# Two-layer graph network: an order of work changed on four engines, and VectorE in place of POOL for the rounding rest of the row tiles

## The chip, the cores and the metric

One NeuronCore of a Trainium2 chip runs the whole program. The metric is the device time of one execution in microseconds (us). Engines are named as in the profile: PE (TensorE; PEld is its weight load), DVE (VectorE), ACT (ScalarE), POOL (GpSimd), SP (the queue that issues the DMAs).

## The reference

```python
edge_index = jnp.stack([src, dst])                     # 80000 edges, 2500 nodes, D = 1024, f32
h = jnp.maximum(_layernorm(x, axis=-1), 0.0)
x = x + _L0_gnn_ref(h, L0_gnn_W, edge_weight, src, dst)
h = jnp.maximum(_layernorm(x, axis=-1), 0.0)
x = x + _L1_gnn_ref(h, edge_index, L1_gnn_W, L1_gnn_b)

# layer 0: support = h @ W; out = segment_sum(support[src] * edge_w[:, None], dst)
# layer 1: edges plus one self loop for each node; h' = h @ W.T + b;
#          deg = number of edges by row; norm = deg^-0.5[row] * deg^-0.5[col];
#          out = segment_sum(norm[:, None] * h'[col], row)
```

`dst` is sorted; `src` is random.

## The kernel before, in words

Both layers are done as dense f16 products, with every operand split into a rounded half and the rest ("first" and "second" part), so that three products give nearly f32. The 2500 rows are 20 row tiles (t = 0 to 19) of 128.

**Layer 0, first half: "supports" and "quads".** For each row tile, PE computes `support(t, k0, k1)`: 8 blocks k of 6 matmuls 128x512 (L1688). Between blocks 1 and 2 it turns the next row tile (`transpose_rows(t + 1)`, L1671, 16 transposes), which needs the rounded half of it (ACT, `rows_normal`, L1470) and the rest, h minus its rounded half (`h_left`, L737, on POOL, counted by `h_ready`). From t = STEP0 = 4 on a tile also carries a quad w = t - 4: sums of one-hot products (L1700) that turn the edge list into dense blocks of the weighted adjacency and of the edge counts. A quad has 8 one-hot steps (w = 0), 4 (w = 1, 2), 3 (w = 3 to 8) or 2 (from w = 9). For a step, POOL fills `fbuf` (L769, L771; `fields_of`), DVE compares and multiplies it into `slots` (L1055 to L1061; `hots_of(w, i0, i1)`, two buffers), and PE multiplies. At a quad's end ACT copies the sums out (L1418 to L1420), DVE makes the second part (L1124 to L1128, `early_second_part`) and SP parks the result in DRAM. In these tiles DVE also does `sup_left` (L962, the support's rest), `split_left` (L1136, the rest of W1 at 2^n scale, t = 4 to 11), `moments` and `scale_shift` of later row groups (L873 to L887), and the table of what edges each later window holds: `own_select` (t = 7, 8 and 10 to 15), `select_windows` (t = SELECT_AT = 9) and `later_windows` (t = TABLE_AT = 16), each of them a chain of small instructions at a tile's end. PE's part of the table is `tables(t)`, after block 5. W1's scale needs its largest absolute row sum: ACT sums (`weight_sums(1, k)`, L1497), DVE reduces (L1032), PE turns it (`spread_max(2, ...)`, L1631), DVE reduces again (L1232), PE spreads it (`to_all(3, ...)`, L1636), DVE makes the power of two.

**Layer 0, second half.** For each target tile, 120 matmuls of adjacency by support (L1801) in 8 groups, the next tile's quads between them.

**Layer 1.** SP loads x1, layer 0's output, in groups of 4 row tiles (`load_x1`, L597) and the edge counts, turned on the way (`load_first_parts`, L587, first parts in `area`; `load_second_parts`, L592, in `etab` and `slots`). ACT makes relu of the norm (L1609), ACT or DVE the rounded half, DVE the rest (`split`, L1302, `h2_ready`). PE: `sums_of_first` for column chunk c = 0 (320 matmuls, L1888), then `products(0)` (L1948), then `sums` and `products` for c = 1 to 4. DVE's `sums2_left` (L1345) makes the sums' second part, on which `products` waits; `norms` (L1363, L1365) is 40 multiply-adds into `s_acc`, one for each of 20 first and 20 second parts of the counts, on which PE waits (`acc_ready`) after the first output tile.

Every engine's program is written out by hand, in order, with semaphores; nothing is reordered.

Of the kernel before, what the change touches and what calls it, by code (L numbers as in the profile page):

```python
# [6 lines left out]
def gnn_two_layers(nc, x, src, dst, edge_weight, w0, w1, b1, out):  # L7
# [5 lines left out]
    P = 128  # L13
# [56 lines left out]
    with ctx:  # L70
# [394 lines left out]
        def _(sp):  # L465
# [62 lines left out]
            for w in range(PQ):  # L528
# [12 lines left out]
                if w + STEP0 == TABLE_AT + 1:  # L541
                    sp.wait_ge(own_ready, len(OWN_AT))
                    sp.wait_ge(table_ready, 2)
                    fetch_parked(0)
# [78 lines left out]
            load_first_parts(0, 0)  # L623
            for s in range(2):
                sp.wait_ge(x1_out[s], 16 * last)
            for k in range(4):
                sp.wait_ge(sup_free, k + 1)
                load_x1(k)
                load_first_parts(0, k + 1)
                if k == 0:  # L630
# [7 lines left out]
            store_x1(last, 1, LAST)  # L638
            sp.wait_ge(x1_out[1], 16 * (T // 2))
# [53 lines left out]
        def _(pool):  # L693
# [120 lines left out]
            for t in range(STEP0, T):  # L814
                if t + 2 < T:
                    h_left(t + 2)
# [40 lines left out]
        def _(dve):  # L857
# [135 lines left out]
            sup_left(1)  # L993

# [3 lines left out]
            def passes(a, b, count, cum, spare, start=None):  # L998
# [7 lines left out]
                if start is not None:  # L1006
                    chain(nc.vector.tensor_scalar(cum, cum, start, None, ALU.add))
                for v0, v1, per, n0 in ((a, min(b, VB), QPT, a // QPT), (max(a, VB), b, 4, QB)):
# [12 lines left out]
            passes(0, VA, n_row[:, 0:VA], wcum[:, 0:VA], wtmp0)  # L1021
# [7 lines left out]
            moments(3)  # L1029
            scale_shift(3)  # L1030
            dve.wait_ge(w1_summed, KD)
            nc.vector.tensor_reduce(top[:, 3:4], w_sums[:, 1, :], AX.X, ALU.max).then_inc(top_ready, 1)  # L1032
            regs = [dve.alloc_register(f"dve_window{i}") for i in range(2)]
# [105 lines left out]

            def support_share(w):  # L1140
                if w in MOMENTS_AT:
                    moments(MOMENTS_AT[w])
# [83 lines left out]
            def later_windows():  # L1226
                chain(nc.vector.tensor_copy(wcum[:, 0:NA], tab[:, 1, VA:NW]))
                passes(VA, NW, wcum[:, 0:NA], wcum[:, 0:NA], wtmp, top[0:1, 10:11])

            hots_of(0)  # L1230
            dve.wait_ge(top_tp, 3)
            nc.vector.tensor_reduce(top[0:1, 5:6], bank[0][0:1, 0:P], AX.X, ALU.max).then_inc(top_row, 1)  # L1232
            dve.wait_ge(top_all, 3)
            powers(bank[1][:, 0:1], 0, 1)
            nc.vector.tensor_scalar(scale_of[:, 0:1], sc[:, 8:9], 2.0 ** 13, None, ALU.mult).then_inc(w_pow, 1)
            for w in range(PQ):
                hots_of(w, 1, 2) if w > 0 else None
                sup_left(w + STEP0 - 1)
                hots_of(w, 2, 8)
                for g in W1_AT.get(w + STEP0, ()):  # L1240
                    split_left(g)
                if w + STEP0 == HOTS_AT:
                    chunk_one_hots()
                further(w, 2)
# [4 lines left out]
                if w + STEP0 in OWN_AT:  # L1249
                    own_select(w + STEP0)  # L1250
                if w + STEP0 == SELECT_AT:
                    select_windows()
                if w + STEP0 == TABLE_AT:
                    later_windows()
# [95 lines left out]
            def norms(c, k0, k1):  # L1350

                for k in range(k0, k1):
                    if k % HK == 0:
                        dve.wait_ge(cthi_in[k // HK], 16 * (c + 1))
                    if k % LK == 0:
                        dve.wait_ge(ctlo_in[k // LK], 16 * (c + 1))
                    for part_of in (ct_hi_of, ct_lo_of):
# [10 lines left out]
                if k1 == T:  # L1368
# [24 lines left out]
            dve.wait_ge(b_in, 16)  # L1393
            for c in range(NCK):
                step = T // KD + 1
                if c == 0:
                    norms(c, 0, T - 6)
                for f in range(KD):
                    sums2_left(c, f)
                    if c > 0:  # L1400
                        norms(c, min(T, step * f), min(T, step * (f + 1))) if step * f < T else None
                if c == 0:
                    norms(c, T - 6, T)
# [4 lines left out]
        def _(act):  # L1408
# [130 lines left out]
            for t in range(T):  # L1539
# [14 lines left out]
                if t in (2, 3):  # L1554
                    act.wait_ge(w1nat_in, 16)
                    for k in range((t - 2) * KD // 2, (t - 1) * KD // 2):
# [68 lines left out]
        def _(pe):  # L1625
# [205 lines left out]
            for t in range(T):  # L1831
                w = t - STEP0
                quad = 0 <= w < PQ
                support(t, 0, 2)
                if t + 1 < T:
                    transpose_rows(t + 1)
                if w == 0:
                    pe.wait_ge(ranges_ready, 2)
# [150 lines left out]
```

## Time and profile before

| | |
|---|---|
| median of 3 runs | 1492.66 us (1488.78 to 1494.58) |
| the profiled execution | 1490.92 us, of which 1489.1 us is the span from its first to its last instruction |
| mean granted TensorE clock | 0.989 of full speed |
| busy share of the span | PE 96%, PEld 57%, DVE 60%, ACT 34%, POOL 30% |
| first row tile to the last quad | 31 to 327 us of the span |
| layer 0's second half | 327 to 917 us |
| layer 1 | 926 us to the end |

[...] A PE line with an idle time in brackets says how long PE stood before it and who released it. Matmul durations in a merged row are those of the group, modelled ends included.

### The profile page before, as it was taken

To read this page: it belongs to the slowest core of one execution; us is meant where nothing else is said; L and a number is where in the kernel's file an instruction comes from. 1 tells how busy PE (TensorE), PEld (TensorE's weight loads), DVE (VectorE), ACT (ScalarE), POOL (GpSimd) and SP (SyncE) were. 2 spreads that over 40 slices of the span, in tenths; PEclk is the share of its full clock that TensorE was granted. 3 is DMA by queue.
4 is the path that set the end of the run, shared out by engine and by line. 5 is a ranking of instruction groups with operands and counts; after the bars stand their busy time and mean duration, and the time that the engine had idled before them with its cause. 6 is when DMAs were issued, how large, how long until landed. Compare 5 with 4: busy or idle time off the path is not lost.

```text
span 1489.1 us, 23949 instructions
## 1 busy us (share of the span) xinstructions
PE 1424.4 (96%) x7586; PEld 846.5 (57%) x7587; DVE 899.7 (60%) x1804; ACT 507.8 (34%) x922; POOL 453.1 (30%) x865
## 2 busy tenths in 40 slices
PE   3989999999999999999999997989999999999999
PEld 2445455456666666666676664446446446446455
DVE  7788785653777776677767662873552452542542
ACT  7545555522444445455455541610000000000000
POOL 2247565432555555555555550000000000000000
PEclk9999999999999999999999998999999999999999
DMA  8303443251544535454545558937308008017002
GB/s 308 114 20 60 105 89 36 28 83 49 97 79 71 96 72 104 86 96 80 109 75 92 100 95 139 264 91 155 98 9 217 29 19 206 29 33 193 29 2 83
DMA packets 427818, 139.14 MB, mean 93 GB/s; under 512 B 397705, under 2 KB 409993, under 8 KB 427669
## 3 DMA queue, kind: packets, MB, share of 16 engines
q1 hardware_dynamic: 427669, 137.43, 42.0%
q8 instruction: 60, 0.98, 0.3%
q14 instruction: 89, 0.73, 0.2%
HBM read 53.46 MB, written 53.52 MB: 72 GB/s over the span
## 4 chain that ended last, share of the span: by engine, by line
PE 67%; issue 12%; DVE 6%; SPq 5%; POOL 4%; DMA 2%; POOLq 2%; ACT 1%; ACTq 0%; DVEq 0%
PE pair L1801 24%; PE pair L1888 18%; PE pair L1948 14%; PE pair L1688 6%; PE pair L1700 4%; SPq L587 3%; DVE own_w L1365 1%; POOLq L766 1%; DMA h<-in_L_gnn_W 1%; SPq L592 1%; POOL deg_acc L787 1%; POOL fbuf L769 1%; POOL fbuf L771 1%; DMA x_scratch<-xt 1%; POOL fbuf L780 1%
## 5 line engine op out<-in xcount | busy, mean ns | idle before, releaser
L1801 PE MATMUL pair<-h,area 128*128 128x512 f16 x2400 | 542.7, 379 | 0.0
L1801 PEld LDWEIGHTS pair<-h,area 128*128 128x128 f16 x2400 | 342.9, 147 | 147.3
L1888 PE MATMUL pair<-area,h 128*128 128x500 f16 x1600 | 340.7, 376 | 9.6 <-DVE h L1302 9.4
L1888 PEld LDWEIGHTS pair<-area,h 128*128 128x128 f16 x1600 | 157.0, 98 | 192.5 <-issue 13.6
L787 POOL TENSOR_TENSOR deg_acc<-deg_acc,area 128x320 f32<-128x320 f32 x160 | 139.7, 873 | 276.0 <-DVE area L1124 274.5
L1948 PE MATMUL pair<-wmat,area 128*125 128x512 f16 x960 | 211.5, 382 | 4.5 <-DVE area L1345 4.5
L1418 ACT ACTIVATE area<-pair 128x320 f32<-128x320 f32 x160 | 70.1, 438 | 329.8 <-PE pair L1700 327.6
L1622 ACT ACTIVATE area<-pair,sc 128x500 f16<-128x500 f32 x40 | 27.1, 677 | 450.0 <-PE pair L1888 450.0
L1948 PEld LDWEIGHTS pair<-wmat,area 128*125 128x125 f16 x960 | 131.7, 138 | 81.7 <-issue 7.3
L792 POOL TENSOR_TENSOR aux<-area,aux 128x320 f16<-128x320 f32 x144 | 147.6, 1025 | 0.0
L1700 PE MATMUL pair<-slots 128*128 128x120 f16 (+1 forms) x1152 | 112.5, 235 | 20.4 <-DVE slots L1061 18.0
L1055 DVE TENSOR_TENSOR slots<-iota_r,fbuf 128x320 f16<-128x320 f16 (+1 forms) x145 | 60.6, 418 | 116.2 <-POOL fbuf L781 47.5
L1425 ACT ACTIVATE aux<-area 128x320 f16<-128x320 f32 x144 | 126.4, 878 | 0.1
L1700 PEld LDWEIGHTS pair<-slots 128*128 128x128 f16 x1152 | 84.7, 99 | 67.5 <-DVE slots L1061 34.7
L1688 PE MATMUL pair<-wmat,aux 128*128 128x512 f16 x480 | 116.0, 391 | 3.1 <-DVE wmat L949 3.1
L1688 PE MATMUL pair<-wmat,xt 128*128 128x512 f16 x480 | 113.1, 386 | 0.3 <-DVE h L962 0.3
L1128 DVE TENSOR_TENSOR area<-area 128x320 f16<-128x320 f16 x160 | 109.6, 685 | 5.5
L1124 DVE TENSOR_TENSOR area<-area 128x16 f16 (+1 forms) x160 | 32.8, 205 | 115.6 <-ACT area L1420 114.6
L1345 DVE SCALAR_TENSOR_TENSOR area<-pair,sc,area 128x500 f16<-128x500 f32 x40 | 28.9, 737 | 120.2 <-ACT area L1622 120.2
L1057 DVE TENSOR_TENSOR slots<-iota_r,fbuf 128x1024 f16<-128x1024 f16 x145 | 99.7, 688 | 0.0
L1688 PEld LDWEIGHTS pair<-wmat,aux 128*128 128x128 f16 x480 | 46.4, 100 | 54.3 <-issue 8.5
L1125 DVE SCALAR_TENSOR_TENSOR area<-pair,area 128x320 f16<-128x320 f32 x160 | 76.8, 480 | 0.0
(208 smaller groups left out, 1263.4 us busy)
## 6 DMA issues: line engine op xcount, KB each, us to landing
c_scratch<-aux SPq DMA_DIRECT2D x72, 320.0 KB, 4.5
xt<-in_x SPq DMA_DIRECT2D x19, 512.0 KB, 3.6
x_scratch<-xt SPq DMA_DIRECT2D x19, 512.0 KB, 4.7
xt<-x_scratch SPq DMA_DIRECT2D x20, 448.0 KB
out_x<-xt SPq DMA_DIRECT2D x19, 448.0 KB
h<-x_scratch SPq DMA_DIRECT2D x4, 2048.0 KB, 10.3
h<-in_x SPq DMA_DIRECT2D x5, 1024.0 KB, 6.2
h<-in_L_gnn_W SPq DMA_DIRECT2D x4, 1024.0 KB, 11.4
```

The costliest lines, as they stand in the source:

```text
L787: pool.tensor_tensor(deg_acc[:], deg_acc[:], c_stage(s), ALU.add).then_inc(win_sum, 1)
L792: pool.tensor_tensor(second_parts, by_source(c_stage(s)), first_parts, ALU.subtract).then_inc(c_lo, 1)
L1057: nc.vector.tensor_tensor(part(to, 0, P), columns(8, P), by_touch(s, 1, 8, P), ALU.is_equal)
L1125: nc.vector.scalar_tensor_tensor(by_window(parts[:, 1], r), sums_in(pair, r, 1), A_DOWN, by_window(parts[:, 0], r), ALU.mult, ALU.subtract ...
L1128: nc.vector.tensor_tensor(parts[:, 1], parts[:, 1], seconds, ALU.add).then_inc(win_lo, 1)
L1418: act.activation(by_window(c_stage(s), r), sums_in(pair, r, 0), ACT.Copy, scale=C_DOWN)
L1425: act.activation(to, by_source(c_stage(s)), ACT.Copy).then_inc(c_hi, 1)
L1688: last = pe.matmul(dest[:, half * H:(half + 1) * H], h_t(t)[:, q, k, :], wmat[:, r, k, half * H:(half + 1) * H], start=k == q == r == 0, s ...
L1700: return pe.matmul(dest, touches[:, t, 0:P], touches[:, t, P:], start=first, stop=last, skip_group_check=True)
L1801: last = pe.matmul(sum_pair(e)[:, half * H:(half + 1) * H], wts(e)[:, q, :, k], hpart(k, r)[:, half * H:(half + 1) * H], start=k == q == r ...
L1888: ins = pe.matmul(sums_of(c, f), hpart(k, q)[:, f * P:(f + 1) * P], counts, start=first and q == 0, stop=last and q == 1, skip_group_check ...
L1948: last = pe.matmul(out_pair(m)[0:RW, half * H:(half + 1) * H], agg_of(k, q)[:, b * RW:(b + 1) * RW], wmat[:, r, k, half * H:(half + 1) * H ...
```

## The change

It reorders work on SP, DVE, ACT and PE and moves one operation from POOL to DVE. The diff is cut: of `passes`, only how it is divided is shown.

```diff
@@ SP, quads
-                if w + STEP0 == TABLE_AT + 1:
+                if w + STEP0 == TABLE_AT + 2:
                     sp.wait_ge(own_ready, len(OWN_AT))
                     sp.wait_ge(table_ready, 2)
                     fetch_parked(0)
@@ SP, end of layer 0
             sp.wait_ge(c_out[1], 32 * (T - PRE))
-            load_first_parts(0, 0)
             for s in range(2):
                 sp.wait_ge(x1_out[s], 16 * last)
             for k in range(4):
                 sp.wait_ge(sup_free, k + 1)
                 load_x1(k)
-                load_first_parts(0, k + 1)
-                if k == 0:
+                load_first_parts(0, k)
+                if k == 1:
                     sp.wait_ge(deg_out, 16)
...
             load_x1(4)
             store_x1(last, 1, LAST)
+            load_first_parts(0, HJ - 1)
@@ POOL, quads
             for t in range(STEP0, T):
-                if t + 2 < T:
-                    h_left(t + 2)
@@ DVE, before the quads
             sup_left(1)
+            moments(3)
...
-            def passes(a, b, count, cum, spare, start=None):
+            def steps_each(a, b, count, cum, spare, start=None):
...
+            def steps_by_quad(a, b, cum, spare):
...
             for t in range(2, STEP0 - 1):
                 sup_left(t)
-            moments(3)
-            scale_shift(3)
             dve.wait_ge(w1_summed, KD)
             nc.vector.tensor_reduce(top[:, 3:4], w_sums[:, 1, :], AX.X, ALU.max).then_inc(top_ready, 1)
+            scale_shift(3)
...
+            def h_left(t):
+
+                dve.wait_ge(relu_ready, 2 * t + 2)
+                dve.wait_ge(ht_tp, 2 * (t - 1))
+                dve.wait_ge(h_ready, t)
+                nc.vector.tensor_tensor(hs(t)[:, 1, :], h[:, t, :], hs(t)[:, 0, :], ALU.subtract).then_inc(h_ready, 1)
...
+            def table_share(t):
+
+                if t in OWN_AT:
+                    own_select(t)
+                if t == SELECT_AT:
+                    select_windows()
+                if t == TABLE_AT:
+                    chain(nc.vector.tensor_copy(wcum[:, 0:NA], tab[:, 1, VA:NW]))
+                    steps_each(VA, NW, wcum[:, 0:NA], wcum[:, 0:NA], wtmp, top[0:1, 10:11])
+                if t == TABLE_AT + 1:
+                    steps_by_quad(VA, NW, wcum[:, 0:NA], wtmp)
@@ DVE, quads
-            hots_of(0)
             dve.wait_ge(top_tp, 3)
             nc.vector.tensor_reduce(top[0:1, 5:6], bank[0][0:1, 0:P], AX.X, ALU.max).then_inc(top_row, 1)
+            hots_of(0, 0, 1)
             dve.wait_ge(top_all, 3)
...
+            hots_of(0, 1, 2)
             for w in range(PQ):
                 hots_of(w, 1, 2) if w > 0 else None
                 sup_left(w + STEP0 - 1)
                 hots_of(w, 2, 8)
+                table_share(w + STEP0 - 1)
                 for g in W1_AT.get(w + STEP0, ()):
                     split_left(g)
                 if w + STEP0 == HOTS_AT:
                     chunk_one_hots()
+                if w + STEP0 + 2 < T:
+                    h_left(w + STEP0 + 2)
                 further(w, 2)
                 if w + 1 < PQ:
                     hots_of(w + 1, 0, 1)
                 early_second_part(w)
                 support_share(w)
-                if w + STEP0 in OWN_AT:
-                    own_select(w + STEP0)
-                if w + STEP0 == SELECT_AT:
-                    select_windows()
-                if w + STEP0 == TABLE_AT:
-                    later_windows()
@@ DVE, layer 1 (norms takes parts: first, second or both)
-            dve.wait_ge(b_in, 16)
+            norms(0, 0, T, (ct_hi_of,))
             for c in range(NCK):
                 step = T // KD + 1
-                if c == 0:
-                    norms(c, 0, T - 6)
                 for f in range(KD):
                     sums2_left(c, f)
-                    if c > 0:
-                        norms(c, min(T, step * f), min(T, step * (f + 1))) if step * f < T else None
+                    if c == 0:
+                        norms(c, f, f + 1, (ct_lo_of,))
+                    elif step * f < T:
+                        norms(c, min(T, step * f), min(T, step * (f + 1)))
                 if c == 0:
-                    norms(c, T - 6, T)
+                    norms(c, KD, T, (ct_lo_of,))
+                    dve.wait_ge(b_in, 16)
@@ ACT
-                if t in (2, 3):
+                if t == 2:
                     act.wait_ge(w1nat_in, 16)
-                    for k in range((t - 2) * KD // 2, (t - 1) * KD // 2):
+                    for k in range(KD):
                         weight_sums(1, k)
@@ PE
                 support(t, 0, 2)
+                if w == 0:
+                    to_all(3, bank[1][:, 0:1], 5, 6)
                 if t + 1 < T:
                     transpose_rows(t + 1)
-                if w == 0:
-                    pe.wait_ge(ranges_ready, 2)
-                    spread_max(2, P, 3)
                 for k in range(2, KD):
                     support(t, k, k + 1)
...
+                    if w == -1 and k == 5:
+                        pe.wait_ge(ranges_ready, 2)
+                        spread_max(2, P, 3)
                     if w == 0 and k == 2:
-                        to_all(3, bank[1][:, 0:1], 5, 6)
                         pe.wait_ge(table_ready, 1)
```

## Rows read from the trace of the kernel before

**Rows 1.** Busy time by stretch: PE, PEld, DVE, ACT, POOL, granted clock, DMA share, GB/s
```profile
84.00:124.00 40.00, 33.86 (x234) 18.68 (x233) 32.28 (x82) 16.98 (x28) 20.82 (x57) 0.91 0.10 32
124.00:168.00 44.00, 44.00 (x309) 23.81 (x308) 36.24 (x72) 25.05 (x38) 30.11 (x73) 1.00 0.50 108
...
285.00:305.00 20.00, 15.12 (x87) 7.32 (x86) 19.50 (x35) 7.91 (x13) 11.89 (x29) 0.91 0.44 84
```

**Rows 2.** Who PE waited for, 84 to 330 us: total us, times, longest
```profile
PE pair L1700 <- DVE slots L1061: 13.3, 5, 4.9
```

**Rows 3.** PE in order of time, quads: start, us, line, operands, count, idle before
```profile
90.15 0.38 PE L1636 MATMUL pair<-top,ones 1*128 1x1 f32 x2 [1.23 <-DVE top L1232]
...
91.90 2.77 PE L1688 MATMUL pair<-wmat,aux 128*128 128x512 f16 x6
...
105.64 0.98 PE L1700 MATMUL pair<-slots 128*128 128x120 f16 x8 [2.98 <-DVE slots L1061]
106.71 3.74 PE L1688 MATMUL pair<-wmat,xt 128*128 128x512 f16 x12
...
194.85 0.98 PE L1700 MATMUL pair<-slots 128*128 128x120 f16 x8 [3.14 <-DVE slots L1061]
...
299.39 0.59 PE L1700 MATMUL pair<-slots 128*128 128x120 f16 x8 [4.88 <-DVE slots L1061]
```

**Rows 4.** DVE in order of time, before and in the quads
```profile
75.98 0.24 DVE L1020 CAST area<-area 1x128 int32<-1x128 f32 x1 [4.65 <-DMA area<-wsmall]
...
80.80 4.82 DVE L873 BATCH_NORM_STATS2 stats<-h 128x6 f32<-128x512 f32 x8
...
102.32 2.17 DVE L1055 TENSOR_TENSOR slots<-iota_r,fbuf 128x320 f16<-128x320 f16 x1 [0.32 <-POOL fbuf L771]
...
186.04 0.35 DVE L1219 TENSOR_SCALAR area<-area 128x768 f16<-128x768 f16 x1
...
191.65 2.25 DVE L1060 TENSOR_TENSOR slots<-slots,fbuf 128x320 f16<-128x320 f16 x1
...
287.79 0.66 DVE L1227 CAST area<-area 1x768 f32<-1x768 int32 x1
...
296.90 1.17 DVE L1017 TENSOR_TENSOR area<-area 1x768 int32<-1x768 f32 x1
```

**Rows 5.** POOL in order of time: the first of 14 subtractions from t = 6 on
```profile
102.20 2.12 POOL L737 TENSOR_TENSOR aux<-h,aux 128x1024 f16<-128x1024 f32 x1
```

**Rows 6.** DVE's groups by line and shape, 915 to 1000 us: busy us, mean ns
```profile
L1302 DVE TENSOR_TENSOR h<-aux,h 128x1024 f16<-128x1024 f32 x10 | 12.2, 1224 | 0.2
...
L1365 DVE SCALAR_TENSOR_TENSOR own_w<-area,dinv,own_w 128x500 f32<-128x500 f16 x13 | 9.6, 739 | 0.7
```

**Rows 7.** PE in order of time, layer 1: column chunks 0 and 1
```profile
926.52 70.32 PE L1888 MATMUL pair<-area,h 128*128 128x500 f16 x320 [9.44 <-DVE h L1302]
1001.37 13.05 PE L1948 MATMUL pair<-wmat,area 128*125 128x512 f16 x48 [4.52 <-DVE area L1345]
...
1046.45 67.63 PE L1888 MATMUL pair<-area,h 128*128 128x500 f16 x320
1113.92 10.52 PE L1948 MATMUL pair<-wmat,area 128*125 128x512 f16 x48
```

**Rows 8.** SP's queue in order of time, end of layer 0: start, us of issue
```profile
895.17 0.43 SPq L619 DMA_DIRECT2D deg_scratch<-deg  x1
896.08 9.19 SPq L587 DMA_TRANSPOSE area<-c_scratch  x1
905.39 0.70 SPq L597 DMA_DIRECT2D h<-x_scratch  x1
```

**Rows 9.** DMA issues, 894 to 934 us: count, size, us from issue to landing
```profile
deg_scratch<-deg SPq DMA_DIRECT2D x1, 10.0 KB, 20.1
```

**Rows 10.** ACT in order of time, layer 1's first instruction
```profile
922.72 1.24 ACT L1609 ACTIVATE area<-h,shift,scale 128x1024 f32<-128x1024 f32 x1 [25.93 <-DMA h<-x_scratch]
```

**Rows 11.** DVE in order of time, the first of the 40 sums for `s_acc`
```profile
978.25 0.48 DVE L1363 TENSOR_SCALAR own_w<-area,dinv 128x500 f32<-128x500 f16 x1 [9.41 <-DMA area<-in_L_gnn_b]
```

More of the change, by code:

```diff
@@ L1007, in passes @@
                     chain(nc.vector.tensor_scalar(cum, cum, start, None, ALU.add))
+            def steps_by_quad(a, b, cum, spare):
+                n = b - a
                 for v0, v1, per, n0 in ((a, min(b, VB), QPT, a // QPT), (max(a, VB), b, 4, QB)):
@@ L1020, in _ @@
             chain(nc.vector.tensor_copy(tab[:, 0, 0:VA], lo_row[:, 0:VA]))
-            passes(0, VA, n_row[:, 0:VA], wcum[:, 0:VA], wtmp0)
+            steps_each(0, VA, n_row[:, 0:VA], wcum[:, 0:VA], wtmp0)
+            steps_by_quad(0, VA, wcum[:, 0:VA], wtmp0)
             chain(nc.vector.tensor_copy(top[0:1, 10:11], wcum[:, VA - 1:VA]))
@@ L1224, in select_windows @@
                 dve.sem_inc(left_ready, 1)
-            def later_windows():
-                chain(nc.vector.tensor_copy(wcum[:, 0:NA], tab[:, 1, VA:NW]))
-                passes(VA, NW, wcum[:, 0:NA], wcum[:, 0:NA], wtmp, top[0:1, 10:11])
-            hots_of(0)
+            def table_share(t):
[8 more added lines that the diff above has]
+                    steps_by_quad(VA, NW, wcum[:, 0:NA], wtmp)
             dve.wait_ge(top_tp, 3)
             nc.vector.tensor_reduce(top[0:1, 5:6], bank[0][0:1, 0:P], AX.X, ALU.max).then_inc(top_row, 1)
+            hots_of(0, 0, 1)
             dve.wait_ge(top_all, 3)
@@ L1348, in _, with norms @@
             accs = [0]
-            def norms(c, k0, k1):
+            def norms(c, k0, k1, parts=(ct_hi_of, ct_lo_of)):
                 for k in range(k0, k1):
-                    if k % HK == 0:
+                    if k % HK == 0 and ct_hi_of in parts:
                         dve.wait_ge(cthi_in[k // HK], 16 * (c + 1))
-                    if k % LK == 0:
+                    if k % LK == 0 and ct_lo_of in parts:
                         dve.wait_ge(ctlo_in[k // LK], 16 * (c + 1))
-                    for part_of in (ct_hi_of, ct_lo_of):
+                    for part_of in parts:
                         counts = part_of(k)
@@ L1367, in norms @@
                         ins.then_inc(acc_step, 1)
-                if k1 == T:
+                if k1 == T and ct_lo_of in parts:
                     dve.wait_ge(acc_step, accs[0])
```

## Prediction

> **What bounds the kernel now.** I read the page first: PE is busy nearly all the time, so the time is PE's matmuls plus the places where PE stands. A change of order can only pay at those places. So the second view is busy time by stretch, to find them [rows 1]: from 124 to 168 us PE works all 44.00 us at full clock (1.00), from 84 to 124 it works 33.86 of 40.00 (6.1 idle), from 285 to 305 it works 15.12 of 20.00 (4.9 idle), and both carry a mean granted clock of 0.91, that is, a part of the stretch at 1.2 instead of 2.4 GHz. The third view, who PE waited for [rows 2], puts 13.3 us of the quads on DVE's one-hots. The fourth, PE in order of time [rows 3], gives the single places: 1.23 us for W1's scale, 2.98 at 105.64, 3.14 at 194.85, 4.88 at 299.39. Before and after each, matmuls are slow: 6 products take 2.77 us, 12 take 3.74, where chunk 1 does 48 in 10.52 [rows 7], so 1.3 and 2.6 are their length. So a stall costs itself and 1.0 to 1.5 us at the lower clock. The listed four make 12.2 us, the waits of [rows 2] and the scale's 14.5; with three small ones of 1 us or less the idle time is 16.6, and with the slow stretches (four of 1.0 to 1.5) about 22 us.
>
> Layer 1's beginning has two more places [rows 7]: PE stands 9.44 us before the first sums and 4.52 before the first products; the 320 sums take 70.32 instead of chunk 1's 67.63, the 48 products 13.05 instead of 10.52. That is 12.1 + 7.0 = 19.2 us. The ceiling of the whole change is thus 22 + 19 = 41 us.
>
> **Quads: what holds DVE.** A one-hot instruction of 128x320 took 2.17 us at 102.32 and 2.25 at 191.65 [rows 4]; its like in the same group take 0.3. POOL's subtraction stood beside the first of them, 102.20 to 104.3 [rows 5]. So DVE's instructions with both operands in SBUF wait until POOL's is over. There are 14 of these (t = 6 to 19), each able to cost DVE up to 1.9 us. The change takes them away and gives DVE 14 subtractions of its own; the same shape, f32 and f16 in, f16 out, takes 1.224 us on DVE [rows 6], 17 us in all, against up to 27 saved. DVE is busy 36.2 of 44 us in [rows 1], so it has no large reserve: what counts is where the 1.2 us lie.
>
> The Trainium skill (SBUF — State Buffer, section on the two separate sides) says that DVE and GpSimd share one port pair, held exclusively for a whole instruction, also by a DVE instruction with two SBUF inputs; the trace agrees in DVE's 2.17 us. By that rule the moved subtraction in its turn blocks POOL 1.2 us.
>
> **The tiles one by one**, walked with PE's tile as fixed work (8 blocks of 1.3 us, transposes 0.9, 0.42 a one-hot step, 1.6 to 4.3 the table) and DVE's list in its new order:
>
> *t = 3.* DVE's 4.65 us before 75.98, a wait for a DMA, are filled by the 4.82 us of `moments(3)` [rows 4]; the chain behind comes 0.8 us later, and W1's maximum is ready at about 82 instead of 87.2. `spread_max` now stands after block 5, which PE reaches at 80.2: a new wait of 1.8 us. ACT does 4 more weight sums (1.04 each) in t = 2, so its rows of t = 5 come 2 us later, at 81; PE needs them at 87.7. Covered.
>
> *t = 4.* The scale's wait of 1.23 and its neighbours (1.0 and 0.9) go: `to_all` comes 5 us after its operand. Eight steps end the tile; the last three stand at block 7 and each must wait for its one-hots (1.55 us for four instructions, two buffers), so of the 2.98 us about 1.2 stay. From 82.73 to 106.71 the tile took 24.0; now 18.9 with the wait of t = 3 in it: 5 us, and 1.0 more because the 12 products at 106.71 run at full clock.
>
> *t = 5 to 8.* No wait before, none now: DVE's subtraction for t + 2 is done 0.6 to 2 us before PE's transposes, closest in t = 5.
>
> *t = 9 to 12.* The select chain, from 186.04 to nearly 191 us [rows 4], stood ahead of a one-hot that PE waited 3.14 us for. It now lies in tile 10 behind all of that tile's one-hots. But `own_select(8)` is now inside tile 9, and PE's `tables(9)` waits for it: about 1.3 us. In tile 11, DVE is late from `moments(5)`, another 1.3. The old waits there (1.6 and 3.14, with the slow products behind) made tiles 9 and 10 6.6 us longer than their work; 2.6 are lost again: 4.0.
>
> *t = 13 to 19.* The table of later windows, from 287.79 to 298 [rows 4], stood before the one-hot of the 4.88 us wait. Its first half (about 5 us) goes to tile 17, its second (4, of which POOL's lock is 1.8) to tile 18, both behind the one-hots, where DVE idled for about 6 us a tile. The 4.88 us and about 1.8 of slow products go: 6.7, and 1.2 in tile 13. SP's `fetch_parked(0)` now waits in t = 18 until about 9 us into it; the fetch lands 5 us later, with 9 us left before PE uses it. SP's queue holds `park_counts(13)` back behind it; ACT waits for that, not PE.
>
> Sum: 6.0 + 4.0 + 7.9 = 17.9. I take 15.5, since the two or three new waits of over 1 us may also bring slow products (1 each). Bounds: 9 (the new waits twice as long and slow ones at each) and 20.
>
> **End of layer 0.** SP spends 9.19 us issuing the first transpose of counts before the first load of x1, 896.08 to 905.39 [rows 8]; ACT starts on it at 922.72 after 25.93 us of waiting [rows 10], and PE 3.8 us later. PE's last matmul of layer 0 ends at 917.1. Now the load goes out at about 896.4, when PE has freed the first four blocks. What is unknown is how fast it is: the write of the counts' sums (`deg_scratch`, 10 KB in 4-byte pieces) stands before it in the queue and takes 20.1 us to land, until 915.3 [rows 9]; in that time the transpose trickled too. Lower bound: the load is finished by 905 and PE starts at 917.3, all 12.1 us come back. Upper: nothing moves before 915 and 2 MB at 5 us more land at 920, PE starts at about 924, 2.7 come back. I take 914 for the landing: PE starts at 917.7, waits about 1.5 us more in pieces for the first splits (DVE 1.9 us each), 9.5 to 10 come back. The later loads: SP now waits for the write's landing before x1's third group, at 915; that group lands by 921 and PE wants it at about 945. The stall goes, and DVE's splits are next: 33 us of work in PE's 67. Covered.
>
> Here the skill speaks against it: DMA: Bandwidth & Descriptors, section Specifications, has pieces under 512 B done as read-modify-write; by that rule the write stays slow and in front of the load. That is the second rival below.
>
> **First products.** DVE waited 9.41 us for the bias [rows 11], which it doesn't need for the sums. 28 of the 40 then run at 0.775 us (0.739 and the step, [rows 6]) ahead of `sums2_left(0, 0)`. Now 20 (15.5 us) follow the last split. That ends at about 957 to 960, so they end by 975, and PE gives the first finished sum at about 975. No wait is left: 7.0 us come back. Then 20 second parts, 8 between the `sums2_left` and 12 behind (9.3 us), end at about 996.5; PE reaches that wait at 996. So 0.5 is given back: 6.5.
>
> Sum here 9.5 + 6.5 = 16, from 9 to 19.
>
> POOL's `fields_of`, now no longer queued behind a wait for ACT's rows, the bias wait and `scale_shift(3)` behind the maximum are costed at nothing: POOL's fields wait for DVE's one-hots anyway, the bias lands 17 us before `finish(0)`, and t = 8's rows are needed 30 us later. Without that cover `scale_shift(3)` would cost its 0.5.
>
> **Total.** 15.5 + 16 = 31.5 off the profiled 1490.9 gives 1459.4; the runs' median lies 1.7 above the profiled one, so 1461.
>
> **The rivals.**
> 1. *DVE is too full* (chance 0.17). For: 36.2 of 44 us busy [rows 1], and now 1.2 us more a tile in a row with the chains ahead of it, so that PE's transposes wait in t = 6 to 12. Against: the 2 us waits for POOL go. 1 us in each of 7 tiles: 1468.
> 2. *The first load stays behind the small write* (0.20): landing at 920. 6.5 us of the 9.5 are lost: 1467 to 1468.
> 3. *Both orders find other covers, nothing moves* (0.05): the one-hots' two buffers already set the quads and the loads the rest. Against it stand the 9.44 us. 1490.
> 4. *Slower* (0.03): the subtraction on DVE stands behind a one-hot that waits for PE, which waits for the transposes. It closes a loop that lasts the tile. It decides once each of 14 tiles grows by over 2.25 us (31.5 / 14), DVE's lateness in t = 5 being 2.9 us from where I put it; at 3 us a tile it is 1461 + 42 = 1503.
> 5. The forecast (0.55): 1461, own range 1453 to 1467.
>
> Faster by over 0.5% (7.5 us, about what a measurement of this kernel tells from no change): 0.92; within: 0.05; slower: 0.03. The range is 1452 to 1474: the low end is the ceiling, 41 us off the median of the runs, and the high end takes in rivals 1 and 2 together (1461 + 7 + 6.5).
>
> **What would show it.** No DVE one-hot of over 1.5 us between 100 and 300; the last quad's product at about 310 instead of 327; PE's waits for one-hots under 5 us instead of 13.3; a new PE wait of 1 to 2 us for the maximum near 80 and one in tile 9. The first sums within 3 us of layer 0's end, 67 to 69 us long, the products right behind. It would be wrong if PE's transposes (L1671) wait for DVE, if the load lands after 918, or if the granted clock stays at 0.91 though the waits are gone.

## The result, and the profile after

| | before | after |
|---|---|---|
| median (lowest to highest), 4 runs each | 1493.04 us (1488.78 to 1494.58) | 1466.67 us (1462.03 to 1469.22) |
| the profiled execution and its span | 1490.92, 1489.1 us | 1462.03, 1460.2 us |
| mean granted TensorE clock | 0.989 | 0.998 |

The ratio is 0.9826, with a 95% interval of 0.9801 to 0.9851: faster by 1.7%, or 26.4 us between the medians. The profiled execution after is the fastest of its four, so the spans differ by a little more, 28.9 us, and the account below is of the spans.

Busy time by stretch, after (columns as in [rows 1]):
```profile
84.00:124.00 40.00, 38.37 (x301) 22.12 (x300) 34.35 (x87) 21.81 (x31) 22.38 (x62) 1.00 0.16 37
...
285.00:305.00 20.00, 20.00 (x130) 10.48 (x129) 9.93 (x25) 5.98 (x11) 6.56 (x20) 1.00 0.64 102
```
The two stretches in which PE idled 6.1 and 4.9 us have 1.6 and 0 idle, and the granted clock is 1.00 in both, where it was 0.91.

Who waited for whom, after, 84 to 300 us (total us, times, longest), the answer to [rows 2]:
```profile
POOL fbuf L769 <- DVE slots L1064: 41.3, 22, 5.7
...
PE pair L1717 <- DVE slots L1064: 1.1, 1, 1.1
...
DVE slots L1058 <- POOL fbuf L771: 0.6, 2, 0.3
```
PE's wait for one-hots fell from 13.3 to 1.1 us. The third row has this one for its like in the kernel before, same view and stretch:
```profile
DVE slots L1055 <- POOL fbuf L771: 26.3, 11, 6.1
```
DVE waited 26.3 us for POOL's fields, now 0.6, and it is POOL that waits for a buffer.

PE in order of time, quads, after (columns as in [rows 3]):
```profile
69.51 2.75 PE L1705 MATMUL pair<-wmat,xt 128*128 128x512 f16 x12 [0.25 <-DVE h L960]
...
79.77 0.27 PE L1648 MATMUL pair<-ident,top 128*1 128x128 f32 x1 [1.44 <-DVE top L1034]
...
98.41 0.59 PE L1717 MATMUL pair<-slots 128*128 128x120 f16 x8 [1.15 <-DVE slots L1064]
...
172.30 0.38 PE L1752 MATMUL pair<-area 128*128 128x512 f16 x1 [1.99 <-DVE area L1222]
...
307.21 26.06 PE L1818 MATMUL pair<-h,area 128*128 128x512 f16 x120
```
Three of the waits forecast are there, near the sizes forecast, and 4.88 and 3.14 are gone. Tile 3 begins at 69.51 where it began at 71.48 before; in the other kernels below it begins between 69.5 and 70.8. From there to the first product of the second half it is 237.7 us, before 255.9 (71.48 to 327.39): 18.2 less.

PE in order of time, layer 1, after, beside [rows 7]:
```profile
903.26 56.25 PE L1906 MATMUL pair<-area,h 128*128 128x500 f16 x256 [6.00 <-DVE h L1318]
...
960.25 13.67 PE L1906 MATMUL pair<-area,h 128*128 128x500 f16 x64 [0.74 <-issue]
973.75 10.52 PE L1966 MATMUL pair<-wmat,area 128*125 128x512 f16 x48
985.52 1.03 PE L1975 MATMUL pair<-ones,own_w 128*125 128x1 f32 x8 [1.25 <-DVEq L1386]
986.42 31.27 PE L1966 MATMUL pair<-wmat,area 128*125 128x512 f16 x144
```
The products follow the sums without a gap, at full clock. The first sums still start 6.00 us after layer 0's last matmul (897.26), and they take 70.7 us from first to last, 70.3 before. From layer 0's end to the products' second part it was 98.2 us (917.1 to 1015.3) and is 89.2 (897.26 to 986.42): 9.1 less.

The account: 2.0 from the earlier start, 18.2 in the quads, 9.1 at layer 1's start make 29.3; 0.4 is lost in layer 0's second half (590.1 us for 589.7). The forecast had 15.5 and 16 for the two terms. Not all of the 29.3 is the change's: the earlier start of tile 3 stands in kernels without the new orders too (69.5 and 69.6 in experiments 3 and 4), and 3.4 of the 9.1 went with a write that landed 3.4 us sooner in this execution, as shown below.

SP's queue, after, the answer to [rows 8]:
```profile
875.24 0.43 SPq L619 DMA_DIRECT2D deg_scratch<-deg  x1
876.27 2.16 SPq L597 DMA_DIRECT2D h<-x_scratch  x1
878.49 20.68 SPq L587 DMA_TRANSPOSE area<-c_scratch  x1
```
ACT in order of time, after, layer 1's first instruction, the answer to [rows 10]:
```profile
899.45 1.24 ACT L1626 ACTIVATE area<-h,shift,scale 128x1024 f32<-128x1024 f32 x1 [22.50 <-DMA h<-x_scratch]
```
DMA, 874 to 914 us, after: what was moved in each of 40 slices of 1 us, and the write's landing, the answer to [rows 9]:
```profile
GB/s 156 178 383 180 15 0 0 45 16 33 20 49 57 16 33 53 66 53 66 176 414 410 399 251 89 227 231 242 389 418 426 406 277 217 191 3 3 31 90 393
...
deg_scratch<-deg SPq DMA_DIRECT2D x1, 10.0 KB, 16.7
```
The load is the second row of SP's queue, issued at 876.3, right behind the write of 10 KB. While the write is under way the engines move at most 66 GB/s from 878 on; it lands at 891.9, in the slice from 894 they move 414, and the 2 MB are there by 899.4. The load was brought forward, and what it had waited for before, it waited for again: ACT starts 7.5 us behind the write's landing here, and started 7.4 behind it before (915.3 to 922.72).

### The profile page after: what moved, and what is told of

Same layout as the page of the kernel before. It is cut to its first block, busy times and chain, and to the rows that moved or that the text cites. A ratio compares the mean times of both kernels' runs of the same rounds, so it can differ in the third digit from the quotient of the medians.

```text
span 1460.2 us, 23951 instructions
## 1 busy us (share of the span) xinstructions
PE 1413.4 (97%) x7586; PEld 842.6 (58%) x7587; DVE 898.2 (62%) x1818; ACT 507.6 (35%) x922; POOL 438.7 (30%) x851
## 4 chain that ended last, share of the span: by engine, by line
PE 81%; issue 8%; DVE 5%; DMA 2%; POOL 2%; ACT 1%; SPq 0%; POOLq 0%; ACTq 0%; DVEq 0%
PE pair L1818 25%; PE pair L1906 23%; PE pair L1966 13%; PE pair L1705 12%; PE pair L1717 4%; DMA h<-x_scratch 2%; PE pair L1765 1%; PE pair L1688 1%; DVE stats L871 1%; DVE own_w L1381 1%; POOL deg_acc L787 1%; POOL fbuf L780 0%; DVE area L981 0%; POOL fbuf L781 0%; ACT aux L1514 0%
## 5 line engine op out<-in xcount | busy, mean ns | idle before, releaser
L1058 DVE TENSOR_TENSOR slots<-iota_r,fbuf 128x320 f16<-128x320 f16 (+1 forms) x145 | 56.7, 391 | 102.2 <-POOL fbuf L781 47.8
L1705 PE MATMUL pair<-wmat,aux 128*128 128x512 f16 x480 | 112.9, 383 | 3.1 <-DVE wmat L947 3.1
L1127 DVE TENSOR_TENSOR area<-area 128x16 f16 (+1 forms) x160 | 38.0, 237 | 107.3 <-ACT area L1437 104.5
L769 POOL CAST fbuf<-etab 128x12 f16 (+6 forms) x146 | 57.4, 393 | 66.1 <-DVE slots L1064 41.3
```

The lines of the kernel that those rows point to most:

```text
L1705: last = pe.matmul(dest[:, half * H:(half + 1) * H], h_t(t)[:, q, k, :], wmat[:, r, k, half * H:(half + 1) * H], start=k == q == r == 0, s ...
```

## The experiments

Open after the result: which part of the change is worth how much, since the quads gave more than I took; whether the write holds the load back; and what of the costs put at nothing was a gain. "The quads" below is the time from tile 3's first product to the first product of the second half: 255.9 us before, 237.7 after. Three later kernels (experiments 5, 6 and 7) have the changed kernel's quads as they are and take 237.6, 237.9 and 237.5, so a difference of 1 us in them can be read from one execution. Whole spans scatter more: the four executions of the kernel after have 1460.2 to 1467.4. Where there is one execution, the reading goes by rows.

**1. The orders without the move.** The kernel after, with the 14 subtractions back on POOL.
```diff
@@ POOL, quads
             for t in range(STEP0, T):
+                if t + 2 < T:
+                    h_left(t + 2)
@@ DVE, quads
-                if w + STEP0 + 2 < T:
-                    h_left(w + STEP0 + 2)
```


> The changed kernel with the 14 subtractions back on POOL, all orders as changed. Theory A (POOL's subtraction holds DVE's one-hots back by 1.9 us each, and where they then come late PE waits): one-hots of over 2 us are back, PE waits for one-hots rise from 6.2 us to 9 to 13 us, the last quad ends at 311 to 315 us instead of 307.2, the time is 4 to 8 us above the changed kernel. Rival (the new orders alone took the one-hots off PE's path, the subtraction's place is worth nothing): the quads end at 306 to 309 us. The end of layer 0 is as in the changed kernel in both.

Measured: 1476.28 us (1473.49 to 1478.49, 4 runs; the kernel before on the same chip 1487.44), ratio 0.9913 (0.9888 to 0.9937), span 1476.7. PE in order of time, orders only:
```profile
101.35 0.98 PE L1710 MATMUL pair<-slots 128*128 128x120 f16 x8 [2.98 <-DVE slots L1066]
...
179.23 0.58 PE L1745 MATMUL pair<-area 128*128 128x512 f16 x1 [3.48 <-DVE area L1217]
...
239.48 0.59 PE L1710 MATMUL pair<-slots 128*128 128x120 f16 x8 [2.12 <-DVE slots L1066]
...
322.08 23.11 PE L1811 MATMUL pair<-h,area 128*128 128x512 f16 x106 [0.69 <-DVE area L1130]
```
The 2.98 us are as long as before, a new wait of 2.12 takes the place of old ones, and DVE waits 28.3 us for POOL's fields. The quads take 251.5 us: 4.4 less than before, 13.8 more than after. By the ratios this kernel is 0.9% slower than the changed one, some 13 us, where I had expected 4 to 8, and the last quad ends at 322 us instead of 311 to 315. The orders alone are worth much less than I had expected, the move more. The rival is out.

**2. The move without the orders.** The kernel before, with only the subtraction moved.
```diff
@@ POOL, quads
-                if t + 2 < T:
-                    h_left(t + 2)
@@ DVE, quads, behind the one-hots
                     chunk_one_hots()
+                if w + STEP0 + 2 < T:
+                    h_left(w + STEP0 + 2)
```


> The kernel before with the 14 subtractions on DVE and no order changed. Theory A: the waits at 105.6 and 194.9 us fall by about 1.8 us each with slow products behind them, the wait for the scale and the one for the table of later windows (4.9 us, less the lock's 1.8) stay; the last quad ends at 319 to 323 us instead of 327.4. Rival (DVE too full without the orders): the quads end at 327 us or later, with PE's transposes waiting for DVE.

Measured: 1471.88 us (1469.98 to 1472.47, 4 runs), ratio 0.9885 (0.9861 to 0.9909), span 1470.7. PE in order of time, move only:
```profile
285.16 0.59 PE L1707 MATMUL pair<-slots 128*128 128x120 f16 x8 [0.42 <-DVE slots L1059]
...
311.48 26.06 PE L1808 MATMUL pair<-h,area 128*128 128x512 f16 x120
```
The first row is the place of the 4.88 us of [rows 3]. `later_windows` still stands ahead of that one-hot, in its old place, and PE waits 0.42. The quads take 240.7 us, 15.2 less. DVE waits 1.7 us for POOL's fields. So the chain of the table needed no other place; DVE had to come to it earlier. The forecast was wrong here too: the second half starts at 311.5, not at 319 to 323, and of the wait for the table I had let 3.1 us stand. The two parts are not a sum in the quads (4.4 and 15.2 against 18.2 together): they clear some of the same waits.

**3. POOL's order alone.** The kernel before, the subtraction still on POOL, but with the sum of counts and the next quad's first two field steps ahead of it. It tells whether the subtraction cost by its work (2.1 us and DVE's blocked one-hot) or by its place, where POOL waits for ACT's rows while DVE wants fields.
```diff
@@ POOL, quads
-                if t + 2 < T:
-                    h_left(t + 2)
                 w = t - STEP0
...
+                if w + 1 < PQ:
+                    fields_of(w + 1, 0, 2)
+                if t + 2 < T:
+                    h_left(t + 2)
...
-                        fields_of(w + 1)
+                        fields_of(w + 1, 2, 8)
```


> The kernel before with one change on POOL: the sum of counts and the first two field steps of the next quad stand ahead of the subtraction of each row tile, which stays on POOL. The lock of 1.9 us stays, the queueing of the fields behind POOL's wait for ACT's rows goes. The quads (from tile 3's first product to the first adjacency product) took 255.9 us before, 241.0 with the subtraction moved. Theory C (much of the move's gain is that the fields no longer queue behind a wait for ACT; DVE waited 26.3 us for them): DVE's wait for fields falls under 10 us, the quads take 246 to 251 us. Rival (the lock is all): 254 to 256 us though DVE waits less for fields.

Measured, one execution: span 1472.2, the quads 243.2 us, 12.7 less than before with no work moved, and more than the 5 to 10 expected. DVE waits 3.8 us for L771 instead of 26.3, and 1.6 for L769. PE in order of time shows the price, transposes that wait for the later subtraction:
```profile
104.57 1.07 PE L1673 MATMUL pair<-ident_u,aux 128*128 128x128 f16 x16 [0.58 <-POOL aux L737]
...
133.24 1.07 PE L1673 MATMUL pair<-ident_u,aux 128*128 128x128 f16 x16 [0.98 <-POOL aux L737]
...
312.68 26.06 PE L1803 MATMUL pair<-h,area 128*128 128x512 f16 x120
```
The run doesn't leave DVE's blocked one-hots as they were: from 84 to 330 us 8 one-hot instructions took over 2 us before, and here 4. So it shows that the work need not be moved, not that the place alone brings 12.7.

**4. The work gone, the wait kept.** The move-only kernel, with POOL still waiting where it waited.
```diff
@@ POOL, quads
+                if t + 2 < T:
+                    pool.wait_ge(relu_ready, 2 * (t + 2) + 2)
+                    pool.wait_ge(ht_tp, 2 * (t + 1))
                 w = t - STEP0
```


> The kernel before with the subtractions on DVE, while POOL keeps its two waits (for ACT's rows and PE's transposes) at the old places and does nothing there. The lock goes, the queueing stays (2.1 us shorter a tile). Theory C: DVE's wait for fields is 12 us or more, the quads take 244 to 249 us. Rival (the lock is all): 241 us, as with the subtraction moved and no waits.

Measured, one execution: span 1470.7, the quads 242.3 us, 13.6 less than before and 1.6 more than with the move alone. Who waited for whom, 84 to 300 us, in this kernel:
```profile
DVE slots L1056 <- POOL fbuf L771: 11.1, 12, 1.9
PE pair L1710 <- DVE slots L1062: 5.5, 4, 1.9
```
The wait alone makes DVE late by up to 1.9 us a tile, which DVE's spare time nearly covers. I had expected 244 to 249 us, and 241 if the work were all; the 242.3 lies nearer to the rival. With experiment 3: changing the place or taking away the work brings 12.7 or 13.6 of the 15.2. I read them as one chain, first the wait for ACT, then 2.1 us of subtraction, then the fields, of which DVE can take one but not both. How the 13.6 divides between DVE's blocked one-hots and fields that come 2.1 us sooner, no run separates.

SP's order at the end of layer 0 is the old one here. PE, layer 1's first sums, this kernel:
```profile
907.64 55.74 PE L1898 MATMUL pair<-area,h 128*128 128x500 f16 x256 [6.00 <-DVE h L1312]
```
The wait is as long as in the kernel after, though the load stands where it stood before. The write took 16.2 us to land.

**5. The small write out of the first load's way.** The kernel after, with the write issued behind the second load of x1, and read back later.
```diff
@@ SP, end of layer 0
-            sp.wait_ge(deg_ready, 1)
-            sp.dma_start(deg_dram.rearrange("t p -> p t"), deg[:, 0:T], allow_slow_non_contiguous=True).then_inc(deg_out, 16)
...
                 if k == 1:
+                    sp.dma_start(deg_dram.rearrange("t p -> p t"), deg[:, 0:T], allow_slow_non_contiguous=True).then_inc(deg_out, 16)
+                if k == 3:
                     sp.wait_ge(deg_out, 16)
```


> The changed kernel with the write of the counts' sums (10 KB in 4-byte pieces) put behind x1's second load instead of ahead of the first, its read back behind the fourth. Theory B (the small write holds every load behind it until it has landed, 16.7 us): the first load lands within 9 us of its issue, ACT starts on it by 886 us instead of 899.5, PE starts the first sums within 1 us of layer 0's last product, the sums take 68 us instead of 70.5; 6 + 2.5 = 8.5 us less than the changed kernel, 1453 to 1455. Rival (the loads are slow because the transposes of counts and the loads share the queue, whatever stands first): the first load still lands 15 us or more after its issue and the time stays at 1460 to 1464.

Measured, one execution: 1468.00 us, span 1466.2, where the four of the kernel after lie between 1460.2 and 1467.4. ACT, this kernel:
```profile
884.70 1.25 ACT L1627 ACTIVATE area<-h,shift,scale 128x1024 f32<-128x1024 f32 x1 [7.22 <-DMA h<-x_scratch]
...
917.04 2.37 ACT L1627 ACTIVATE area<-h,shift,scale 128x1024 f32<-128x1024 f32 x2 [16.17 <-DMA h<-x_scratch]
```
PE, this kernel:
```profile
897.62 30.52 PE L1907 MATMUL pair<-area,h 128*128 128x500 f16 x144
931.23 23.77 PE L1907 MATMUL pair<-area,h 128*128 128x500 f16 x112 [3.08 <-DVE h L1319]
...
961.72 16.51 PE L1907 MATMUL pair<-area,h 128*128 128x500 f16 x64 [6.72 <-issue]
```
The first load is there at 884.7, 8 us after its issue at 876.6, and the sums start with no wait. But the write (17.9 us to land) now stands ahead of the third load and the counts behind it, and PE waits 3.08 us for a split of that load. For the 6.72 us the row names no releaser; the counts that those sums need were loaded behind the write, too. From layer 0's end to the products' second part it is 93.1 us (897.62 to 990.74), after 89.2. The mechanism is shown: the third load takes 23.8 us from its issue (893.2) where the first took 8. My time was wrong: I had moved the hold, not removed it.

**6. The write made fast, in its place.** The kernel after; PE turns the sums (128x20 to 20x128), DVE copies them out, and SP writes 20 rows of 512 B instead of 2560 pieces of 4 B.
```diff
@@ SP, end of layer 0
-            sp.wait_ge(deg_ready, 1)
-            sp.dma_start(deg_dram.rearrange("t p -> p t"), deg[:, 0:T], allow_slow_non_contiguous=True).then_inc(deg_out, 16)
+            sp.wait_ge(deg_rows_ready, 1)
+            sp.dma_start(deg_dram, deg_rows).then_inc(deg_out, 16)
@@ PE, last target tile
+                if g == 1:
+                    pe.wait_ge(deg_ready, 1)
+                    pe.transpose(TP[0:T, 0:P], deg[:, 0:T], ident[:]).then_inc(deg_tp, 1)
@@ DVE
+            dve.wait_ge(deg_tp, 1)
+            nc.vector.tensor_copy(deg_rows, TP[0:T, 0:P]).then_inc(deg_rows_ready, 1)
...
```


> The changed kernel with the counts' sums turned by PE (one transpose of 128x20 in layer 0's last tile) and copied by DVE, so that the same 10 KB go out at the same place as 20 rows of 512 bytes. Theory B, with the piece size as the cause: the write lands within 4 us, the first load goes out about 2 us later than in the changed kernel and lands within 9 us, PE starts the first sums within 1 us of layer 0's end; 1453 to 1455. If not the size but any write there is the cause: landing 10 us or more, 1460 to 1464.

Measured, one execution: 1453.46 us, span 1451.7, 8.5 less than the lowest of the four after. ACT, turned sums:
```profile
887.57 1.24 ACT L1631 ACTIVATE area<-h,shift,scale 128x1024 f32<-128x1024 f32 x1 [10.13 <-DMA h<-x_scratch]
```
PE, turned sums:
```profile
897.68 67.69 PE L1914 MATMUL pair<-area,h 128*128 128x500 f16 x320
965.21 10.52 PE L1974 MATMUL pair<-wmat,area 128*125 128x512 f16 x48
```
The load, issued at 879.6, is there 8 us later; the stall of 6.0 us is gone and with it 3.0 us in the sums (70.7 to 67.7). Of these, 0.7 was a gap inside the sums (at 960.25) and the rest the lower clock behind the stall: after, the granted clock is 0.54 from 903 to 908 and 1.00 from 908 to 920, and here it is 1.00 from 897 to 965. From layer 0's end to the products' second part it is 80.2 us (897.68 to 977.88), after 89.2.

**7. The sums for `s_acc` in the old order.** The kernel after, with all of chunk 0's sums behind the bias wait again, 28 of them ahead of `sums2_left(0, 0)`.
```diff
@@ DVE, layer 1
-            norms(0, 0, T, (ct_hi_of,))
+            dve.wait_ge(b_in, 16)
...
+                if c == 0:
+                    norms(c, 0, T - 6)
                 for f in range(KD):
                     sums2_left(c, f)
-                    if c == 0:
-                        norms(c, f, f + 1, (ct_lo_of,))
...
```


> The changed kernel with the 40 sums for column chunk 0 in their old order (after the wait for the bias, 28 of them ahead of the first second part). Theory: this order alone made the 4.5 us wait before the first products and the slow products behind it; both are back, the 48 products take 13 instead of 10.5 us, the time is 6 to 7.5 us above the changed kernel's 1460.2 span; the quads as in the changed kernel. Rival (the wait went because the loads, the bias with them, come earlier): a wait of under 1.5 us and no slow products.

Measured, one execution: span 1465.7, between those of the four of the kernel after; the rows tell more. PE, this kernel:
```profile
977.90 11.97 PE L1965 MATMUL pair<-wmat,area 128*125 128x512 f16 x48 [3.80 <-DVE area L1361]
990.98 1.03 PE L1974 MATMUL pair<-ones,own_w 128*125 128x1 f32 x8 [1.10 <-DVEq L1386]
```
DVE in order of time, this kernel, the first of the 40 sums:
```profile
954.79 0.48 DVE L1379 TENSOR_SCALAR own_w<-area,dinv 128x500 f32<-128x500 f16 x1 [9.71 <-DMA area<-in_L_gnn_b]
```
3.80 of wait and 1.45 of slow products make 5.3; from the first sums to the products' second part it is 88.4 us, after 83.2, and the forecast was 6 to 7.5. The rival is out: the bias is no earlier, it comes 51.3 us behind the first sums here and came 51.7 behind them before. The run puts back both the wait for the bias and the sums ahead of `sums2_left(0, 0)`, and doesn't tell them apart.

**8. What the runs point to.** Experiment 6, with the three new waits of the change taken up: `own_select(8)` behind tile 9's second one-hots, `spread_max` one block later, and two second parts of the counts ahead of the first `sums2_left`.
```diff
@@ DVE, quads
+                if w + STEP0 == SELECT_AT:
+                    table_share(SELECT_AT - 1)
                 sup_left(w + STEP0 - 1)
                 hots_of(w, 2, 8)
-                table_share(w + STEP0 - 1)
+                if w + STEP0 != SELECT_AT:
+                    table_share(w + STEP0 - 1)
@@ DVE, layer 1
             norms(0, 0, T, (ct_hi_of,))
+            norms(0, 0, 2, (ct_lo_of,))
@@ PE
-                    if w == -1 and k == 5:
+                    if w == -1 and k == 6:
...
```


> The changed kernel with the counts' sums turned by PE (1451.7 span alone) and three orders: the select chain's first part (own_select of tile 8) right behind tile 9's second one-hots instead of behind all of them (takes away PE's 1.99 us in tile 9), PE turns W1's maximum after block 6 instead of 5 (1.46 to about 0.2), two of the 20 second sums ahead of the first second part (the 1.25 us before PE's counts product go). Expected: span 1446 to 1449, ratio to the kernel before 0.970 to 0.974. If each wait only moves to the next tile: 1451 to 1453.

Measured: 1450.20 us (1449.15 to 1450.57, 5 runs; before on that chip 1488.17), ratio 0.9745 (0.9731 to 0.9759), span 1448.6, granted clock 1.0. PE in order of time, this kernel:
```profile
80.93 0.27 PE L1657 MATMUL pair<-ident,top 128*1 128x128 f32 x1 [0.19 <-DVE top L1037]
...
172.63 0.59 PE L1726 MATMUL pair<-slots 128*128 128x120 f16 x8 [0.76 <-DVE slots L1067]
...
306.01 26.06 PE L1827 MATMUL pair<-h,area 128*128 128x512 f16 x120
```
The maximum's wait fell from 1.44 to 0.19, tile 9's from 1.99 to 0.76 and to another place, and the quads to 235.4; the products run from 963.70 on with no wait ahead of their second part, where experiment 6 still had one of 1.26. The span is 3.1 us below experiment 6, in the range forecast (1446 to 1449), and this is the fastest of these kernels.

## Why the prediction was right, and where not

The forecast was 1461 and the median 1466.67, in its range and 5.7 above it; of 31.5 us forecast, 26.4 came between the medians and 28.9 between the profiled spans. That is right as a whole, with one of its two terms right and the other too large. In part the nearness is luck: of the 28.9 us, 2.0 are the earlier start of tile 3 and 3.4 the faster landing of the small write, and no run puts either down to an edit. Without them it is 23.5, 8 us short of the forecast.

**The quads' walk held, tile by tile.** PE's transposes start 2.0 us earlier than before in tile 3 (72.09 for 74.07), 8.2 in tile 5 (102.06 for 110.29), 8.2 in tile 9 (163.24 for 171.46), 12.7 in tile 13 (220.69 for 233.36), and the first product of the second half 20.2 earlier. So tiles 3 and 4 gave 6.2 (forecast 6.0), tiles 5 to 8 nothing (nothing), tiles 9 to 12 gave 4.5 (4.0), tiles 13 to 19 gave 7.5 (7.9). The waits forecast at 1.8 in tile 3, 1.2 in tile 4 and 1.3 in tile 9 measured 1.44, 1.15 and 1.99; that of 1.3 in tile 11 did not come. The sum of the walk was 17.9 and the quads gave 18.2. The deduction to 15.5, for slow products behind the new waits, was not needed in this execution: the 12 products behind the wait in tile 4 took 2.75 us, full speed, with 1.15 us of wait ahead of them. It was no empty fear, as the last section shows.

**The reason given for it was half of it.** I argued with DVE's one-hots blocked beside POOL's subtraction. That is there: no 128x320 one-hot instruction of over 1.1 us is left, and the two multiplications, 514 and 531 ns in the mean before, take 350 and 314. DVE's groups, 100 to 300 us, after:
```profile
L1063 DVE TENSOR_TENSOR slots<-slots,fbuf 128x320 f16<-128x320 f16 x40 | 14.0, 350 | 0.0
...
L1064 DVE TENSOR_TENSOR slots<-slots,fbuf 128x320 f16<-128x320 f16 x40 | 12.6, 314 | 0.0
```
The same two groups before:
```profile
L1061 DVE TENSOR_TENSOR slots<-slots,fbuf 128x320 f16<-128x320 f16 x39 | 20.7, 531 | 0.0
L1060 DVE TENSOR_TENSOR slots<-slots,fbuf 128x320 f16<-128x320 f16 x39 | 20.0, 514 | 0.0
```
But over the three groups of 128x320 one-hots that is 41.2 us for 55.2, 14 saved, and some 3 more in `split_left` (939 ns in the mean before, 742 after), against 17 of subtractions taken on: DVE's work is about the same. What counts is where it lies, and there a step that I "costed at nothing" counts, POOL's `fields_of` no longer queued behind a wait for ACT's rows. My cover, that fields wait for DVE's one-hots anyway, was true of POOL at one time of a tile and untrue at another: the chain of waits shows DVE waiting 26.3 us for those fields. Experiment 3 gets 12.7 us with the subtraction still on POOL, so the move of the work is not needed for most of the gain; experiment 4 gets 13.6 with the wait still there, so by itself the step costed at nothing is worth 1.6. And `later_windows`, to which I put 6.7 us, lay harmless in its old place once DVE was early (experiment 2). The sum was right because my walk had DVE's lateness in it, not because each edit bore the price beside its name.

**The end of layer 0 failed at one step: "I take 914 for the landing"**, 3 us ahead of layer 0's end. The load landed 2.2 us behind it (899.4 to 897.26), before 5.6 behind it (922.7 to 917.1). So 3.4 us of the wait came back, and nothing of the slow clock, where the term had 9.5. Even the 3.4 is not the order's: the write took 16.7 us to land instead of 20.1, 3.4 less, and the load was there 7.5 us behind its landing, before 7.4. The kernels of experiments 2, 3 and 4 have SP's old order, with the write landing in 16.8, 18.1 and 16.2 us, and PE waits 6.68, 7.39 and 6.00 us there. So no run shows any gain from the load's new place as long as the slow write stands ahead of it. That is rival 2, which had 0.20, and it was priced too low: "2 MB at 5 us more land at 920", where the rows of the kernel before already had 7.4 us between the write's landing and the load's, which gives 922.7 again and nothing back. Experiments 5 and 6 show that the write ahead of the load is the cause. I had seen the sign, the transpose trickling beside the write, and chose a value in the middle between two mechanisms, where there is nothing: either the load passes the write or it doesn't. Right behind it stands the rule cited with that rival (the Trainium skill, DMA: Bandwidth & Descriptors, Specifications: pieces under 512 B done as read-modify-write). The runs agree in that behind the same 10 KB in pieces of 512 B the load takes 8 us from its issue, and behind pieces of 4 B some 15 us longer; that the cause is read-modify-write and not the number of pieces (2560 against 20) no run here shows.

**The first products** held: 4.52 us of wait and 2.5 of slow clock came back, 7.0, and experiment 7 gives 5.3 of them to the order of the sums, the bias wait included. The kernels of experiments 2, 3 and 4, with the old order there, still wait 4.43, 4.77 and 4.84 us. The `acc_ready` wait was 1.25 us instead of 0.5, so 5.8 instead of 6.5.

**The other rivals.** DVE too full (1): false, no transposes waited for DVE, and PE idled 1.6 us from 84 to 124. Nothing moves (3) and slower (4): false; DVE's subtraction never closed the loop.

**Open:** why tile 3 starts up to 2 us earlier or later from kernel to kernel, why the same small write takes between 16.2 and 20.1 us to land, and why a short wait of PE is followed by the lower clock in one execution and not in the next (last section).

## What to carry to other kernels

A wait on an in-order engine costs what is queued behind it, so before pricing an engine's work, look who waits for its next instructions; moving a few of them ahead of the wait may bring most of what moving the work does (here 12.7 us of 15.2). Bringing a DMA forward in its queue brings nothing if a slow one still stands ahead: look what the DMA engines move in that time, and make the slow one cheap (here a 128x20 turn on PE) rather than passing it on to the next load. A chain that seems to set a wait may be innocent if its engine merely came to it late; test its place by itself. Before a shorter wait is credited to an edit, look for it in a kernel that lacks the edit.

## What the runs showed of the hardware

A write of 10 KB in pieces of 4 B took 16.2 to 20.1 us to land, in every kernel that had it, and a load of 2 MB right behind it in SP's queue took 22.5 to 23.8 us from issue; with nothing slow ahead the same load took 8. In the kernel after the engines moved at most 66 GB/s from 878 us until the landing, and 414 in the slice from 894.

A short wait of PE was followed by the lower clock in some executions and not in others. Ahead of the second part of layer 1's first products PE waits 1.25 or 1.26 us in the kernel after and in experiments 1, 5 and 6. The 144 products then take 31.27 us in the kernel after and in experiment 6, but 32.96 in experiments 1 and 5 (in 1 the granted clock is 0.60 from 1001 to 1005 us, 1.00 from there to 1034). PE in order of time, experiment 1:
```profile
1001.18 32.96 PE L1959 MATMUL pair<-wmat,area 128*125 128x512 f16 x144
```

The exclusion between DVE and POOL goes both ways. POOL in order of time, after:
```profile
154.26 4.55 POOL L769 CAST fbuf<-etab 128x6 f16 x1
158.77 0.19 POOL L771 TENSOR_TENSOR fbuf<-etab,area 128x2 f16<-128x2 f16 x1
```
DVE in order of time, after, the end of the same stretch:
```profile
154.92 1.40 DVE L1139 SCALAR_TENSOR_TENSOR aux<-h,sc,aux 128x512 f16<-128x512 f32 x2
156.24 1.21 DVE L1148 TENSOR_TENSOR aux<-h,aux 128x1024 f16<-128x1024 f32 x1
...
158.22 0.31 DVE L1063 TENSOR_TENSOR slots<-slots,fbuf 128x320 f16<-128x320 f16 x1
158.45 0.31 DVE L1064 TENSOR_TENSOR slots<-slots,fbuf 128x320 f16<-128x320 f16 x1
```
POOL's small cast, whose like takes 0.2 to 0.3 us, ends at 158.8, when DVE's unbroken run of instructions with two operands in SBUF does, which began at 154.12. The spans of POOL are rough, but the start of the next instruction agrees. So DVE may hold POOL not for one instruction, as I had put it (1.2 us), but for a whole run of them. Two more casts took 4.45 us (at 172.03) and 2.71 (at 126.30), and both end with such a run too. Before, no cast of the quads was longer than 1.7 us. Here POOL had the time: it waits 41.3 us for DVE's buffers.
